# Pre-LN transformer layer on eight cores: per-tile tokens for the transposed activations, and the softmax scaling moved from VectorE to ScalarE

## The chip, the cores and the metric

The kernel runs as one program on all 8 cores of one Trainium2 chip (two dies, cores 0 to 3 and 4 to 7). The metric is the device time of the slowest core in microseconds (us). Each core has a matrix engine (TensorE, PE in the rows; PEld are its weight loads), VectorE (DVE), ScalarE (ACT), GpSimd (POOL), and SyncE (SP), which issues transfers.

## The reference

One layer with layer norm ahead of each half, cut to its core (4 sequences of 2048 tokens, width 2048, 16 heads of 128, 16 experts of width 1024, top 4, and a shared expert):

```python
x = x + attn(layernorm(x))        # scores = q k^T * 128**-0.5, causal, softmax, probs @ v, then @ Wo + bo
x = x + moe(layernorm(x))         # sigmoid router, top 4 renormalised, silu(x wg) * (x wu) @ wd, plus shared expert
```

The softmax is `exp(s) / sum(exp(s))` over the keys of a row. The division by the row sum is the scaling that this case moves.

## The kernel before

Two cores share one sequence. Each core takes 1024 query rows (every second row), and builds keys and values for all 2048 rows of its sequence. Weights are cast to bf16 on their way in. The program is four blocks of hand-ordered instructions. A small scheduler class (`Sched`) keeps one in-order list per engine and a table of tokens: an operation names the tokens it reads and writes, and gets a semaphore wait for the last writer of each token it reads (and for the readers of each token it writes). Nothing is reordered: what stands first in an engine's list runs first.

**Block 1, layer norm and transposes** (about 0 to 111 us). 16 tiles of 128 rows are loaded, normalised (`ln1_stats`, `ln1_norm`, L269 on ScalarE), transposed on TensorE into the four PSUM tiles `psLN` (`ln1_tp`, L280) and copied by VectorE into `ln1T` (`ln1_ev`, L288). All 32 copies write one token, `("lnT",)`.

**Block 2, attention** (about 112 to 1173 us). For each of 16 heads, `projall` (through `proj`, L347) makes q, k and v with 2 + 4 + 4 groups of 16 matmuls of 512 columns; ScalarE evicts each group (L351). `vtrans` transposes v (L459, L463). Then 8 query tiles k = 0 to 7 follow. Tile k has L = 256(k+1) keys, so L runs from 256 to 2048, in chunks of 512 or 256. For one tile:

- `s_front(k)`: per chunk a TensorE matmul into one of three banks of `psS` (L368), a VectorE minimum and mask in place (L376, L381, L386), and a ScalarE exp into `psb[k % 3]` (L391), whose row sum is read out by a second ScalarE instruction (ACTIVATION_READ_ACCUMULATOR, same line).
- `s_back(k)`: on VectorE the sum of the chunk sums (L404), the reciprocal (L407), and then the scaling of the whole row block `psb`, 128 x L, by the reciprocal, in place (L411).
- `pt_part(k)`: 2(k+1) TensorE transposes of `psb` into `psPT` (L424), evicted by ScalarE copies of up to 1024 columns into `ptb` (L429).
- `pv_part(k)`: 2(k+1) TensorE matmuls with v (L437); every fourth tile a ScalarE copy to `YT` (L444).

The tiles are software-pipelined by the order in which they are listed:

```python
for k in range(NST):
    s_front(k)
    if k >= 1: s_back(k - 1)
    if k >= 2: pt_part(k - 2)
    if k >= 3: pv_part(k - 3, h)
s_back(7)
if h + 1 < NH: projall(h + 1)      # and the prefetch of weights for head h + 2
pt_part(6); pv_part(5, h); pt_part(7); pv_part(6, h); pv_part(7, h)
```

**Blocks 3 and 4**: the output projection with `wo` (about 1173 to 1346 us; its weight loads wait for all that the engines did in attention), then the second layer norm with the router and the 17 expert passes (1458 us to the end) in one block. The change touches none of them.

Of the kernel before, what the change touches and what calls it, by code (L numbers as in the profile page):

```python
# [10 lines left out]
AF = mybir.ActivationFunctionType  # L11
ALU = mybir.AluOpType
# [139 lines left out]
def build_program():  # L152
# [22 lines left out]
    S = Sched()  # L175

    with ExitStack() as top:
# [5 lines left out]
        cst = E(nc.sbuf_tensor("cst", [128, 3], F32))  # L183
        onr = E(nc.sbuf_tensor("onr", [1, 128], BF16))
        st_ln = E(nc.sbuf_tensor("st_ln", [128, 16], F32))
        st_at = E(nc.sbuf_tensor("st_at", [128, 24], F32))
        bnr = E(nc.sbuf_tensor("bnr", [128, 48], F32))

        with ExitStack() as sAB:
# [3 lines left out]
            with ExitStack() as s1:  # L193
# [10 lines left out]
                with ExitStack() as p1:  # L204
# [5 lines left out]
                    psLN = [EP(nc.psum_tensor(f"psLN{j}", [128, 1024], BF16)) for j in range(4)]  # L210
# [8 lines left out]
                         writes=[("io32",)])  # L219
                    S.op("dve", lambda e, a=ident, b=io32: e.tensor_scalar(a[:], b[:], 0.0, None, ALU.is_equal),  # L220
                         reads=[("io32",)], writes=[("ident",)])
# [5 lines left out]
                         reads=[("bqtr",)], writes=[("bqts",)])  # L227

                    for nm, dst, src in (("wqb", wqb, d_wq), ("wkb", wkb, d_wk), ("wvb", wvb, d_wv)):
                        S.dma("pool", nm,  # L230
                              lambda e, o=dst, i=src: e.dma_start(out=o[:], in_=i[0], max_dma_last_dim=MDL),
                              writes=[(nm,)])
# [51 lines left out]
                    def ln1_ev(i):  # L284
                        for j in range(2):
                            bj = 2 * (i % 2) + j
                            S.op("dve", lambda e, p=psLN[bj], i=i, j=j:
                                 e.tensor_copy(ln1T[:, 8 * j:8 * (j + 1), i * 128:(i + 1) * 128],  # L288
                                               p[:].rearrange("p (a b) -> p a b", b=128)),
                                 reads=[("psLN", bj)], writes=[("lnT",)])  # L290

                    ln1_load(0)
                    ln1_load(1)
# [14 lines left out]
                    for k in range(NST):  # L308
# [3 lines left out]
                              writes=[("xr", k)])  # L312
# [6 lines left out]
                with ExitStack() as at:  # L319
# [5 lines left out]
                    psb = [EA(nc.sbuf_tensor(f"psb{s}", [128, 2048], BF16)) for s in range(3)]  # L325
# [9 lines left out]
                    def proj(h, wbuf, wtok, bias_ap, btok, scal, dst, dtok, nchunks, pp, stride2):  # L335
                        for ncx in range(nchunks):
                            p = psP[pp[0] % 2]
                            ptok = ("psP", pp[0] % 2)
                            pp[0] += 1
                            fns = []  # L340
                            for ct in range(NCT):
                                if stride2:
                                    rhs = lnr[:, ct, 4 * ncx:4 * ncx + 4, 0:256:2]
                                else:
                                    rhs = ln1T[:, ct, ncx * 512:(ncx + 1) * 512]
                                fns.append(lambda e, p=p, w=wbuf, ct=ct, rhs=rhs:
                                           e.matmul(p[:], w[:, ct, :], rhs,  # L347
                                                    start=(ct == 0), stop=(ct == NCT - 1)))
                            S.group("pe", fns, reads=[(wtok,), ("lnT",)], writes=[ptok])
                            S.op("act", lambda e, p=p, d=dst, ncx=ncx, b=bias_ap, sc=scal:  # L350
                                 e.activation(d[:, ncx * 512:(ncx + 1) * 512], p[:], AF.Identity,  # L351
                                              bias=b, scale=sc),
                                 reads=[ptok, btok], writes=[dtok + (ncx,)])
# [43 lines left out]
                    def s_back(k):  # L397
                        par = k % 2
                        pb = k % 3
                        base = 12 * par  # L400
                        L = 256 * (k + 1)
                        nchunks = len([512] * (L // 512) + ([256] if L % 512 else []))
                        S.op("dve", lambda e, base=base, nchunks=nchunks:
                             e.reduce_sum(st_at[:, base + 9:base + 10], st_at[:, base + 5:base + 5 + nchunks],  # L404
                                          axis=AX.X),
                             reads=[("sum", par, ci) for ci in range(nchunks)], writes=[("tsum", par)])
                        S.op("dve", lambda e, base=base: e.reciprocal(st_at[:, base + 10:base + 11],  # L407
                                                                     st_at[:, base + 9:base + 10]),
                             reads=[("tsum", par)], writes=[("at2", par)])
                        S.op("dve", lambda e, L=L, base=base, pb=pb:  # L410
                             e.tensor_scalar(psb[pb][:, 0:L], psb[pb][:, 0:L],  # L411
                                             st_at[:, base + 10:base + 11], None, ALU.mult),
                             reads=[("at2", par), ("psb", pb)], writes=[("psb", pb)])

                    def pt_part(k):
                        pb = k % 3
# [86 lines left out]
            with ExitStack() as wp:  # L503
# [7 lines left out]
                      writes=[("bo",)])  # L511
                for co in range(2):
# [3 lines left out]
                          writes=[("wob", co)])  # L516
                S.dma("pool", "wg", lambda e: e.dma_start(out=wg_b[:], in_=d_wgt[0], max_dma_last_dim=MDL),
                      writes=[("wg",)])
                S.dma("pool", "wu", lambda e: e.dma_start(out=wu_b[:], in_=d_wut[0], max_dma_last_dim=MDL),
                      writes=[("wu",)])  # L520
                for co in range(4):
                    sl = co % 2
                    if co >= 2:
# [3 lines left out]
                              writes=[("wob", sl)])  # L527
                    for m in range(NST):
                        fns = [lambda e, m=m, ct=ct, sl=sl: e.matmul(psW[m][:], YT[:, ct, m * 128:(m + 1) * 128],  # L529
                                                                     wo_b[sl][:, ct, :],  # L530
                                                                     start=(ct == 0), stop=False)
                               for ct in range(NCT)]
# [4 lines left out]
                                writes=[("psW", m)])  # L537
# [3 lines left out]
                             reads=[("psW", m), ("xr", m)], writes=[("xr", m)])  # L541
                S.flush(nc, semh)

        with ExitStack() as fp:
# [19 lines left out]
                  writes=[("gw",)])  # L564
            for hh in range(2):
# [4 lines left out]
                      writes=[("wd", hh)])  # L570
            S.dma("pool", "smp", lambda e: e.dma_start(out=ebr_sb[:], in_=d_ebr[:], max_dma_last_dim=MDL),
                  writes=[("ebr",)])
            S.level("smp", [("ebr",)])

            with ExitStack() as rp:
# [4 lines left out]
                     reads=[("onr",), ("ebr",)], writes=[("psR",)])  # L580
# [39 lines left out]
                for mt in range(NST):  # L620
# [6 lines left out]
                         reads=[("xr", mt)], writes=[("bnr2", sl, 0)])  # L627
                    S.op("dve", lambda e, x=xv, bb=bb: e.bn_stats(bnr[:, bb + 6:bb + 12], x[:, 512:1024]),  # L628
                         reads=[("xr", mt)], writes=[("bnr2", sl, 1)])
                    S.op("dve", lambda e, x=xv, bb=bb: e.bn_stats(bnr[:, bb + 12:bb + 18], x[:, 1024:1536]),  # L630
                         reads=[("xr", mt)], writes=[("bnr2", sl, 2)])
                    S.op("dve", lambda e, x=xv, bb=bb: e.bn_stats(bnr[:, bb + 18:bb + 24], x[:, 1536:2048]),  # L632
                         reads=[("xr", mt)], writes=[("bnr2", sl, 3)])
                    S.op("dve", lambda e, bb=bb, b=b: e.bn_aggr(st_ln[:, b:b + 2], bnr[:, bb:bb + 24]),
                         reads=[("bnr2", sl, 0), ("bnr2", sl, 1), ("bnr2", sl, 2), ("bnr2", sl, 3)],
                         writes=[c0])
                    S.op("act", lambda e, b=b: e.activation(st_ln[:, b + 2:b + 3], st_ln[:, b + 1:b + 2],  # L637
                                                            AF.Ln, bias=cst[:, 0:1], scale=1.0),
                         reads=[c0, ("cst",)], writes=[c1])
                    S.op("act", lambda e, b=b: e.activation(st_ln[:, b + 3:b + 4], st_ln[:, b + 2:b + 3],  # L640
                                                            AF.Exp, bias=cst[:, 1:2], scale=-0.5),
                         reads=[c1, ("cst",)], writes=[c1])
# [4 lines left out]
                         reads=[c0, c1], writes=[c2])  # L647
                    S.op("act", lambda e, x=xv, b=b:
                         e.activation(lnb2[:], x, AF.Identity, bias=st_ln[:, b + 4:b + 5],  # L649
                                      scale=st_ln[:, b + 3:b + 4]),  # L650
                         reads=[("xr", mt), c1, c2, ("lnb2",)], writes=[("lnb2",)])
                    for j in range(2):
                        fns = [lambda e, p=psL2[j], q=q, j=j:
                               e.transpose(p[:, q * 128:(q + 1) * 128],  # L654
                                           lnb2[:, (8 * j + q) * 128:(8 * j + q + 1) * 128], ident[:])
                               for q in range(8)]
# [4 lines left out]
                             reads=[("pl", j)], writes=[("x2t", mt, j)])  # L661
# [3 lines left out]
            with ExitStack() as xp:  # L665
# [5 lines left out]
                for e_i in range(NE + 1):  # L671
                    shared = (e_i == NE)
                    for th in range(2):
                        for which, wbuf, wtok, ps in (("g", wg_b, ("wg",), psG), ("u", wu_b, ("wu",), psU)):
                            for mi in range(8):
                                p = ps[mi % 2]
                                ptok = (f"ps{which}", mi % 2)
                                fns = [lambda e, p=p, w=wbuf, ct=ct, mi=mi, th=th:
                                       e.matmul(p[:], w[:, ct, mi * 128:(mi + 1) * 128],  # L679
                                                X2T[:, ct, th * 512:(th + 1) * 512],  # L680
                                                start=(ct == 0), stop=(ct == NCT - 1))
                                       for ct in range(NCT)]
# [6 lines left out]
                                if which == "g":  # L689
                                    S.op("act", lambda e, p=p, mi=mi: e.activation(g_sb[:, mi, :], p[:], AF.Silu,  # L690
                                                                                   bias=cst[:, 1:2], scale=1.0),
                                         reads=[ptok, ("cst",)], writes=[("gsb", mi)])
                                else:
                                    S.op("dve", lambda e, p=p, mi=mi: e.tensor_tensor(g_sb[:, mi, :], p[:],  # L694
                                                                                      g_sb[:, mi, :], ALU.mult),
                                         reads=[ptok, ("gsb", mi)], writes=[("gsb", mi)])
                        if th == 1 and e_i <= NE - 1:
                            nsrc_g = d_swgt if e_i == NE - 1 else d_wgt[e_i + 1]
                            S.dma("pool", "wg", lambda e, s=nsrc_g: e.dma_start(out=wg_b[:], in_=s, max_dma_last_dim=MDL),
                                  writes=[("wg",)])  # L700
                        for mtl in range(4):
                            mt = th * 4 + mtl
                            for co in range(4):
                                bnk = (mtl * 4 + co) % 4
                                p = psD[bnk]
                                fns = [lambda e, p=p, ic=ic, mtl=mtl, co=co:
                                       e.matmul(p[:], g_sb[:, ic, mtl * 128:(mtl + 1) * 128],  # L707
                                                wd_b[:, ic, co * 512:(co + 1) * 512],
                                                start=(ic == 0), stop=(ic == 7))
                                       for ic in range(8)]  # L710
                                S.group("pe", fns,
                                        reads=[("gsb", ic) for ic in range(8)] + [("wd", 0), ("wd", 1)],
                                        writes=[("psD", bnk)])
# [115 lines left out]
```

## Time and profile before

| | |
|---|---|
| times of the kernel before | 4324.37 and 4946.24 us; median 4635.31 us |
| the profiled execution, whole | 4326.25 us |
| its span on the slowest core (3) | 4324.6 us |
| TensorE busy | 3889.8 us, 90% of the span |
| VectorE busy | 1018.8 us, 24% |
| ScalarE busy | 802.6 us, 19% |
| GpSimd busy | 88.0 us, 2% |

The times are of one execution each. The profile is a separate execution, and all its rows are of core 3. Busy shares are means over stages that have different limits, so the rows below are of single stages. The other cores' spans are 4304.9 to 4321.6 us. The median stands between two executions that differ by 14%, and the profiled execution agrees with the lower of them.

### The profile page before, as it was taken

Reading aid. Unit: us, or ns where it says so; the run is one execution under the profiler, and the core shown is the slowest. Engines: PE = TensorE matmul, PEld = TensorE weight load, DVE = VectorE, ACT = ScalarE, POOL = GpSimd, SP = SyncE. Lnnn points to the kernel's source line nnn. Section 1 sums busy time; section 2 is a strip of 40 time slices with the busy share of each in tenths; the row PEclk is TensorE's granted clock in tenths of the full one; section 3 lists DMA queues with packets and bytes.
Section 4 is the critical chain, followed back from the end, with each engine's and each line's share of the span. In section 5 each row is a group of like instructions: output and inputs, shape, how many; then the busy total and the mean of one; then the engine's idle time right before and its main releaser. Section 6 shows DMA issues by size and latency. Waiting matters only on the chain.

```text
span 4324.6 us, 50288 instructions; the slowest of 8 cores (4304.9 to 4324.6 us)
## 1 busy us (share of the span) xinstructions
PE 3889.8 (90%) x19553; PEld 1832.6 (42%) x19553; DVE 1018.8 (24%) x1837; ACT 802.6 (19%) x1427; POOL 88.0 (2%) x129
## 2 busy tenths in 40 slices
PE   2888888878674699999999999999999999999999
PEld 2444444444332344444444444444444444444444
DVE  5132232232211221122122112212211221221122
ACT  3355454454401300000000000000000000000000
POOL 0000000000000000000000000000000000000000
PEclk9989889889887799999999999999999999999999
DMA  6311111111192043734725626527437347256261
GB/s 195 84 20 25 25 20 30 25 20 30 17 140 40 1 66 52 117 49 69 117 33 84 98 34 103 81 37 117 65 53 117 49 69 117 33 85 98 34 103 78
DMA packets 74100, 284.41 MB, mean 66 GB/s; under 512 B 2960, under 2 KB 11408, under 8 KB 69776
## 3 DMA queue, kind: packets, MB, share of 16 engines
q0 software_dynamic: 68832, 247.61, 35.6%
q1 hardware_dynamic: 5040, 33.58, 2.2%
q8 instruction: 165, 2.70, 0.2%
q14 instruction: 63, 0.52, 0.0%
HBM read 520.39 MB, written 8.39 MB: 122 GB/s over the span
## 4 chain that ended last, share of the span: by engine, by line
PE 66%; DVE 1%; ACT 1%; DMA 1%; issue 0%; POOL 0%; DVEq 0%; ACTq 0%; POOLq 0%
PE psD L707 22%; PE psG L679 22%; PE psU L679 22%; DMA ebr_sb<-ebr 1%; DVE g_sb L694 1%; ACT lnb L649 0%; PE psL L654 0%; ACT L637 0%; DVE X2T L659 0%; DVE bnr L626 0%; DVE bnr L632 0%; DVE bnr L630 0%; DVE bnr L628 0%; ACT st_ln L637 0%; ACT st_ln L640 0%
## 5 line engine op out<-in xcount | busy, mean ns | idle before, releaser
L707 PE MATMUL psD<-wd_b,g_sb 128*128 128x512 bf16 x4352 | 944.7, 379 | 35.8 <-DVE g_sb L694 35.8
L679 PE MATMUL psG<-X2T,wg_b 128*128 128x512 bf16 x4352 | 947.0, 380 | 0.0
L679 PE MATMUL psU<-X2T,wu_b 128*128 128x512 bf16 x4352 | 944.9, 379 | 0.0
L690 ACT ACTIVATE g_sb<-psG,cst 128x512 bf16<-128x512 f32 x272 | 186.9, 687 | 2611.9 <-PE psG L679 2611.9
L707 PEld LDWEIGHTS psD<-wd_b,g_sb 128*128 128x128 bf16 x4352 | 423.5, 98 | 557.1 <-issue 51.6
L679 PEld LDWEIGHTS psG<-X2T,wg_b 128*128 128x128 bf16 x4352 | 426.2, 98 | 514.9 <-issue 2.8
L679 PEld LDWEIGHTS psU<-X2T,wu_b 128*128 128x128 bf16 x4352 | 425.9, 98 | 513.4
L694 DVE TENSOR_TENSOR g_sb<-psU,g_sb 128x512 bf16<-128x512 f32 x272 | 188.1, 692 | 1682.5 <-PE psU L679 1682.5
L721 DVE SCALAR_TENSOR_TENSOR x_res<-psD,c_all,x_res 128x512 f32<-128x512 f32 x512 | 384.2, 750 | 540.6 <-PE psD L707 540.6
L368 PE MATMUL psS<-kt,qt 128*128 128x512 bf16 (+1 forms) x320 | 136.4, 468 | 116.6 <-ACT psb L391 53.3
L347 PE MATMUL psP<-ln1T,wvb 128*128 128x512 bf16 x1024 | 223.6, 379 | 0.0
L347 PE MATMUL psP<-ln1T,wkb 128*128 128x512 bf16 x1024 | 223.6, 379 | 0.0
L391 ACT ACTIVATE psb<-psS,cst 128x512 bf16<-128x512 f32 (+1 forms) x320 | 206.7, 647 | 49.2 <-DVE psS L386 18.8
L381 DVE SCALAR_TENSOR_TENSOR psS<-psS,mask_sb 128x256 f32<-128x256 f32 x128 | 55.0, 430 | 678.9 <-PE psS L368 670.9
L529 PE MATMUL psW<-wo_b,YT 128*128 128x512 bf16 x512 | 119.6, 388 | 41.8 <-DMA wo_b<-wo 41.8
L429 ACT COPY ptb<-psPT 128x1024 bf16<-128x1024 bf16 (+1 forms) x192 | 152.3, 794 | 12.1 <-PE psPT L424 1.0
L347 PEld LDWEIGHTS psP<-ln1T,wkb 128*128 128x128 bf16 x1024 | 100.1, 98 | 121.2
L347 PEld LDWEIGHTS psP<-ln1T,wvb 128*128 128x128 bf16 x1024 | 100.1, 98 | 120.9
L424 PE MATMUL psPT<-ident,psb 128*128 128x128 bf16 x1152 | 110.1, 251 | 40.8 <-ACT ptb L429 16.4
L347 PE MATMUL psP<-ln1T,wqb 128*128 128x512 bf16 x512 | 128.7, 411 | 1.4 <-PEq L124 1.4
L386 DVE TENSOR_SCALAR psS<-psS 128x512 f32<-128x512 f32 x192 | 127.1, 694 | 9.8 <-PE psS L368 8.0
L437 PE MATMUL psPV<-ptb,vsb 128*128 128x128 bf16 x1152 | 105.0, 246 | 14.8 <-ACT ptb L429 14.8
(95 smaller groups left out, 1137.2 us busy)
## 6 DMA issues: line engine op xcount, KB each, us to landing
wg_b<-wgt POOLq DMA_DIRECT2D x16, 4096.0 KB, 29.3
wu_b<-wut POOLq DMA_DIRECT2D x16, 4096.0 KB, 29.4
wd_b<-wdt POOLq DMA_DIRECT2D x32, 2048.0 KB, 22.9
xsl<-xkv SPq DMA_DIRECT2D x16, 1024.0 KB, 5.1
wqb<-wq POOLq DMA_DIRECT2D x16, 512.0 KB, 5.2
wkb<-wk POOLq DMA_DIRECT2D x16, 512.0 KB, 5.1
wvb<-wv POOLq DMA_DIRECT2D x16, 512.0 KB, 5.1
x_res<-xkv SPq DMA_DIRECT2D x8, 1024.0 KB, 18.9
```

The source lines that it names most:

```text
L347: e.matmul(p[:], w[:, ct, :], rhs, start=(ct == 0), stop=(ct == NCT - 1)))
L368: e.matmul(psS[:, bk * 512:bk * 512 + w], qt[:, k * 128:(k + 1) * 128], kt[:, off:off + w], start=True, stop=True)],
L386: e.tensor_scalar(psS[:, bk * 512:bk * 512 + w], psS[:, bk * 512:bk * 512 + w], 90.0, None, ALU.min),
L391: e.activation(psb[pb][:, off:off + w], psS[:, bk * 512:bk * 512 + w], AF.Exp, bias=cst[:, 2:3], scale=1.0, accum_out=st_at[:, base + 5 + ...
L424: e.transpose(pt[:, (j - r) * 128:(j - r + 1) * 128], psb[pb][:, j * 128:(j + 1) * 128], ident[:])
L429: e.copy(ptb[tb][:, r:r + n, :], pt[:, 0:n * 128].rearrange("p (a b) -> p a b", b=128)),
L529: fns = [lambda e, m=m, ct=ct, sl=sl: e.matmul(psW[m][:], YT[:, ct, m * 128:(m + 1) * 128], wo_b[sl][:, ct, :], start=(ct == 0), stop=Fals ...
L679: e.matmul(p[:], w[:, ct, mi * 128:(mi + 1) * 128], X2T[:, ct, th * 512:(th + 1) * 512], start=(ct == 0), stop=(ct == NCT - 1))
L690: S.op("act", lambda e, p=p, mi=mi: e.activation(g_sb[:, mi, :], p[:], AF.Silu, bias=cst[:, 1:2], scale=1.0), reads=[ptok, ("cst",)], writ ...
L694: S.op("dve", lambda e, p=p, mi=mi: e.tensor_tensor(g_sb[:, mi, :], p[:], g_sb[:, mi, :], ALU.mult), reads=[ptok, ("gsb", mi)], writes=[(" ...
L707: e.matmul(p[:], g_sb[:, ic, mtl * 128:(mtl + 1) * 128], wd_b[:, ic, co * 512:(co + 1) * 512], start=(ic == 0), stop=(ic == 7))
L721: e.scalar_tensor_tensor(x_res[:, mt, co * 512:(co + 1) * 512], p[:], c_all[:, mt, e_i:e_i + 1], x_res[:, mt, co * 512:(co + 1) * 512], AL ...
```

## The change

Two edits. In block 1 each of the 32 copies into `ln1T` now writes the token of its own row tile, and each projection group reads the tokens of the row tiles that its columns come from: tiles 0 to 7 or 8 to 15 for q, four tiles for each group of k and v. In `s_back` the scaling of `psb` by the reciprocal is issued on ScalarE as an Identity activation, with a zero bias from `cst[:, 1:2]` and the reciprocal as its scale, where it was a VectorE multiply.

```diff
@@ ln1_ev @@
-                                 reads=[("psLN", bj)], writes=[("lnT",)])
+                                 reads=[("psLN", bj)], writes=[("lnT", i)])
@@ proj @@
-                            S.group("pe", fns, reads=[(wtok,), ("lnT",)], writes=[ptok])
+                            if stride2:
+                                ln_toks = [("lnT", t2) for t2 in range(8 * ncx, 8 * ncx + 8)]
+                            else:
+                                ln_toks = [("lnT", t2) for t2 in range(4 * ncx, 4 * ncx + 4)]
+                            S.group("pe", fns, reads=[(wtok,)] + ln_toks, writes=[ptok])
@@ s_back @@
-                        S.op("dve", lambda e, L=L, base=base, pb=pb:
-                             e.tensor_scalar(psb[pb][:, 0:L], psb[pb][:, 0:L],
-                                             st_at[:, base + 10:base + 11], None, ALU.mult),
-                             reads=[("at2", par), ("psb", pb)], writes=[("psb", pb)])
+                        S.op("act", lambda e, L=L, base=base, pb=pb:
+                             e.activation(psb[pb][:, 0:L], psb[pb][:, 0:L], AF.Identity,
+                                          bias=cst[:, 1:2], scale=st_at[:, base + 10:base + 11]),
+                             reads=[("at2", par), ("psb", pb), ("cst",)], writes=[("psb", pb)])
```

## Rows read from the trace of the kernel before

**Rows 1.** Busy time by stretch, core 3: stretch, length, busy (count) per engine, granted clock.
```profile
core 3: us, PE busy (x) PEld busy (x) DVE busy (x) ACT busy (x) POOL busy (x), PEclk, DMA share, GB/s
615.40:639.20 23.80, 14.93 (x98) 8.55 (x95) 17.61 (x46) 20.45 (x51) 0.00 (x0) 0.73 0.00 1
639.20:678.90 39.70, 38.74 (x218) 18.79 (x215) 0.99 (x4) 11.34 (x16) 1.59 (x3) 0.99 0.22 39
1458.00:4324.60 2866.60, 2825.74 (x13065) 1275.66 (x13062) 600.23 (x838) 189.77 (x275) 52.04 (x64) 1.00 0.45 74
```
**Rows 2.** Waits of ScalarE, 113 to 1173 us: waiter, waited for, us in total, times, longest.
```profile
ACT psb L391 <- DVE psS L386: 18.8, 32, 0.9
ACT psb L391 <- DVE st_at L404: 5.7, 25, 0.3
```
**Rows 3.** ScalarE in time order within one head: start, duration, instruction, [idle before <-releaser].
```profile
618.40 0.21 ACT L391 ACTIVATION_READ_ACCUMULATOR psb<-psS,cst 128x1 f32 x1
619.56 0.69 ACT L391 ACTIVATE psb<-psS,cst 128x512 bf16<-128x512 f32 x1 [0.95 <-DVE psS L386]
...
622.34 0.69 ACT L391 ACTIVATE psb<-psS,cst 128x512 bf16<-128x512 f32 x1 [0.28 <-DVE st_at L404]
...
623.80 0.69 ACT L391 ACTIVATE psb<-psS,cst 128x512 bf16<-128x512 f32 x1 [0.20 <-DVE psS L386]
...
638.19 0.69 ACT L391 ACTIVATE psb<-psS,cst 128x512 bf16<-128x512 f32 x1 [0.15 <-DVE st_at L404]
```
**Rows 4.** VectorE in time order, same head, same columns.
```profile
618.30 0.16 DVE L407 RECIPROCAL st_at<-st_at 128x1 f32<-128x1 f32 x1
618.57 0.29 DVE L411 TENSOR_SCALAR psb<-psb,st_at 128x256 bf16<-128x256 bf16 x1
618.77 0.69 DVE L386 TENSOR_SCALAR psS<-psS 128x512 f32<-128x512 f32 x1
```
**Rows 5.** Instruction groups by shape: busy us, mean ns of one, idle before.
```profile
L411 DVE TENSOR_SCALAR psb<-psb,st_at 128x2048 bf16<-128x2048 bf16 x16 | 12.1, 753 | 1.7
L411 DVE TENSOR_SCALAR psb<-psb,st_at 128x256 bf16<-128x256 bf16 x16 | 4.6, 286 | 1.7
L269 ACT ACTIVATE lnb<-xsl,st_ln 128x2048 bf16<-128x2048 f32 x16 | 33.3, 2088 | 0.2 <-issue 0.2
L429 ACT COPY ptb<-psPT 128x1024 bf16<-128x1024 bf16 x96 | 96.6, 1006 | 5.0 <-PE psPT L424 1.0 <-ACT ptb L429 0.4
L429 ACT COPY ptb<-psPT 128x256 bf16<-128x256 bf16 x32 | 11.8, 368 | 2.3
```
**Rows 6.** ScalarE in time order, end of block 1: two normalisations back to back.
```profile
104.21 4.07 ACT L269 ACTIVATE lnb<-xsl,st_ln 128x2048 bf16<-128x2048 f32 x2
```
**Rows 7.** End of block 1: line L124 of TensorE's queue, then the timeline around it.
```profile
L124 PEldq EVENT_SEMAPHORE  x4: 51/51/51, 111.5 to 4324.6; - x4
...
110.62 0.69 DVE L288 COPY ln1T<-psLN 128x1024 bf16<-128x1024 bf16 x1 [0.17 <-PE psLN L280]
111.89 7.39 PE L347 MATMUL psP<-ln1T,wqb 128*128 128x512 bf16 x32 [1.39 <-PEq L124]
```
**Rows 8.** Last head, end of attention: ScalarE in time order.
```profile
1164.50 1.73 ACT L429 COPY ptb<-psPT 128x1024 bf16<-128x1024 bf16 x2
1166.56 4.24 ACT L429 COPY ptb<-psPT 128x1024 bf16<-128x1024 bf16 x4 [0.33 <-PE psPT L424]
```
**Rows 9.** q projection on TensorE: slowest and fastest of ten heads, then all (as rows 5).
```profile
172.38 8.92 PE L347 MATMUL psP<-ln1T,wqb 128*128 128x512 bf16 x32
...
837.39 7.39 PE L347 MATMUL psP<-ln1T,wqb 128*128 128x512 bf16 x32
...
L347 PE MATMUL psP<-ln1T,wqb 128*128 128x512 bf16 x512 | 128.7, 411 | 1.4 <-PEq L124 1.4
```
**Rows 10.** Granted clock in 3 us stretches of one head, columns as rows 1.
```profile
633.00:636.00 3.00, 0.75 (x2) 0.19 (x2) 2.04 (x4) 2.83 (x7) 0.00 (x0) 1.00 0.00 0
636.00:639.00 3.00, 2.57 (x22) 2.40 (x23) 1.56 (x5) 2.55 (x9) 0.00 (x0) 0.57 0.00 0
```

## Prediction before the run

> **What bounds the kernel now.** I read the busy time by stretch first, because the page's busy shares are means over stages with different limits. From 1458 us to the end TensorE is busy for 2825.74 of 2866.60 us [rows 1]. The change touches nothing there, so 2867 us of the time cannot move. Attention repeats one head of about 70.5 us, and a head has two halves. In the second, the projections (639.20 to 678.90 us), TensorE is busy for 38.74 of 39.70 us and VectorE for 0.99: this half is TensorE's. In the first, the eight query tiles (615.40 to 639.20 us), TensorE is busy for 14.93 of 23.80 us, VectorE for 17.61 and ScalarE for 20.45. So the engine that receives the moved work is the fullest in the only half in which that work is due.
>
> Busy shares don't prove that ScalarE sets the pace, so I read what it waits for. In the tiles part its two waits for VectorE come to 18.8 + 5.7 = 24.5 us over all of attention [rows 2], 1.5 us a head. In one head these are four gaps, 0.95 + 0.28 + 0.20 + 0.15 = 1.58 us [rows 3]; all else is back-to-back ScalarE work and its own short gaps. The reader is to see that what VectorE could give back by being relieved is at most 24.5 us in all, and that anything put on ScalarE beyond these gaps lengthens the head.
>
> **Edit 1, the tokens.** The first projection could start before the last `ln1T` copies only if nothing else held it. The row in front of it shows what does: it idles 1.39 us, released by TensorE's queue at L124, and not by VectorE; an event semaphore of that line stands at 111.5 us, behind the end of the last copy at 110.62 + 0.69 = 111.31 us [rows 7]. The engines meet at the end of each block (x4, one per block end), so at 111.5 us all 32 copies are done and every new wait is already met. Later heads read copies that are long past. Value 0. If the meeting were not binding, the gain would end at the 1.39 us, so the range is 0 to -1.4 us. No instruction or transfer is added.
>
> **Edit 2, removed from VectorE.** 128 multiplies, 8 a head, from 286 ns (L = 256) to 753 ns (L = 2048) [rows 5]. They are worth only the gaps above.
>
> **Edit 2, added to ScalarE.** 128 activations of 128 x L, bf16 to bf16 in SBUF, with a per-partition scale and bias. The trace has no such instruction on bf16 input. The nearest row is the normalisation L269, with the same function and operand kinds: 2088 ns for 2048 columns [rows 5]. The slope comes from the copies, (1006 - 368) / 768 = 0.831 ns a column [rows 5]. Two L269 in a row end 4.07 us after the first starts, so the second costs 4.07 - 2.09 = 1.98 us [rows 6], which is 1.70 + 0.28. A scaling inserted between other ScalarE work thus costs 0.28 + 0.000831 L us. The low bound takes the copy's fixed part: 0.368 - 0.213 = 0.155 us, less the same 0.1 us of overlap, 0.05 instead of 0.28. I take 0.28, since L269 carries the same operands and the copy carries none.
>
> The Trainium skill ("ScalarE: Activation LUTs", section "What ACT_TABLE_LOAD costs") gives 280 ns + 0.833 ns a column with a pointer bias, 93 ns more for a pointer scale, and an overlap of 93 ns between neighbours. L269 agrees: 2079 ns by that rule, 2088 measured. The same page's "Rules for kernel authors" would leave a multiply on VectorE, in bf16 up to about 3 times faster; the rows give 2088 against 753 ns at 2048 columns, 2.8 times.
>
> **Where the eight scalings of a head fall.** In ScalarE's list `s_back(k-1)` stands behind the exps of tile k, and ahead of the copies of `pt_part(k-2)` and the exps of tile k+1, which wait behind it.
> - k = 0 to 5 fall inside the tiles part. Their columns sum to 256(1+...+6) = 5376: 5376 x 0.831 ns = 4.47, and 6 x 0.28 = 1.68, together 6.15 us a head.
> - k = 6 and 7 (1.77 and 1.98 us) come after the last exp. What follows on TensorE is the projection of the next head, which needs ScalarE first for an eviction some 4 us in, and the projections leave ScalarE 39.70 - 11.34 = 28 us free [rows 1]. Hidden, cost 0, in 15 heads. In the last head no projection covers them: the two copies at 1164.50 wait for the first, the four copies at 1166.56 for both [rows 8], and the barrier and weight loads of `wo` follow. Gross 1.77 + 1.98 = 3.75; 0.33 us of that is idle already, so +3.4 us, once.
>
> **What the gaps give back, a head.** The 0.95 us gap stands where tile 2's first exp waits for VectorE's minimum. The reciprocal ends at 618.30 + 0.16 = 618.46; then VectorE does the multiply, 0.29 us, and only then the minimum from 618.77 to 619.46 [rows 4]. With the multiply gone the minimum starts about 0.28 us earlier, and the k = 0 scaling (0.49 us) runs on ScalarE in the gap that is left (0.95 - 0.28 = 0.67): 0.28 + 0.49 = 0.77 us back. The three small gaps (0.63 us) close, as ScalarE reaches those exps later than before and VectorE sooner. Sum 1.40 us a head; low bound 0.77.
>
> TensorE loses nothing: its transposes of tile k-1 come an iteration later, when the scaling is long done, and its waits in this part are already for ScalarE. The reciprocal is no new wait either: it is ready 0.4 us after the last mask, within the last exp.
>
> **Sum.** 16 x (6.15 - 1.40) = 76.0; plus 3.4 for the last head; plus 0 for edit 1: +79.4 us. On the profiled execution, 4326.25 + 79.4 = 4405.7 us, 1.8% more. The median before, 4635.31 us, is half way to an execution of 4946.24 us, and I predict the undisturbed level of the profiled execution and of the 4324.37 us.
>
> **The clock.** The granted clock is 1.00 at 633 us, where TensorE hardly works, and 0.57 at 636 to 639 us, after that pause [rows 10]; between the levels 1.2 and 2.4 GHz. The q projection starts on it: 7.39 us in the fastest head and 8.92 in the slowest, 128.7 / 16 = 8.04 on average [rows 9]. The pauses of TensorE ahead of the last tile's matmuls grow by the scaling inserted there, so the low clock can be met in more heads. Bounds: all heads as the slowest, 15 x 0.88 = +13 us; all as the fastest, 15 x -0.65 = -10 us. I take 0, as the mean of 8.04 already lies between the two and nothing here says which way the meeting of pause and projection will drift.
>
> **The rivals.**
> - *Dearer.* The same mechanism, but the three small gaps stay (16 x 0.63 = +10) and the projections all start as the slowest (+13): 4405.7 + 23 = 4429 us. For it: TensorE's pauses grow. Against it: VectorE has slack by then. With only 7.1 us more than my sum it passes 2% (4412.8 us).
> - *Cheaper scaling.* The fixed part is the copy's: 16 x 6 x 0.23 = -22, 4384 us. For it: bf16 input from SBUF is not in the rows. Against: the operands are those of L269.
> - *Not slower.* VectorE's queue, not ScalarE, paces the tiles (minimum, mask, sum, reciprocal and multiply lie in one line), and the scalings disappear in ScalarE's slack. It would return the whole 24.5 us: 4326.25 - 24.5 + 3.4 = 4305 us. It needs 6.15 us of slack on ScalarE in each tiles part; it has 23.80 - 20.45 = 3.35, of which 1.58 in waits on VectorE. It decides only where ScalarE has more idle time than the scaling costs.
> - *No effect.* Scalings and gains cancel, 4326 us; this needs the same slack.
>
> **How the numbers follow.** Chances: my sum 0.53; dearer 0.32; cheaper 0.09; not slower or no effect 0.04; anything else 0.02. About 2% is what a measurement of this kernel can tell from no change. My sum, cheaper, and the two rivals without loss lie within it: 0.66, less 0.01 for a gain larger than any mechanism I find. The dearer rival lies beyond it, with half of the unnamed: 0.33. Faster gets 0.02, since even a perfect relief of VectorE is 0.6%. The range is from the cheaper rival less 8 us of clock, 4376, to the dearer plus 9 us for what I mis-sized, 4438. It leaves out the cases without loss.
>
> **What the profile after would show.** VectorE has no L411 and is 66 us less busy (128 at the middle of 286 and 753 ns). ScalarE has 128 Identity activations on `psb`, about 0.60 us at L = 256 and 2.09 at 2048, on average 1.34, some 172 us in all. A tiles part lasts 28.5 us instead of 23.8, a projections part 39.7 as before, a head about 75.3. ScalarE's waits for VectorE nearly vanish, and TensorE's waits for `psb` grow. The first projection still starts behind L124. The stretch of the experts stays 2867 us. I am wrong if the activations come out much under 0.5 us at L = 256, if the tiles part grows by less than the scalings inside it minus 1.6 us, or if the projections part changes length.

## The result

| | before | changed |
|---|---|---|
| median of all runs | 4324.86 us (10 runs) | 4502.98 us (11 runs) |
| lowest run | 4323.95 us | 4416.67 us |
| ratio, changed to before | | 1.0216, 95% interval 1.0202 to 1.0231 |
| profiled execution, span of the slowest core | 4324.6 us | 4416.1 us |
| ScalarE busy | 802.6 us | 958.0 us |
| VectorE busy | 1018.8 us | 953.9 us |

The change makes the kernel 2.2% slower, about 93 us on 4325. Seven of the eleven executions of the changed kernel had one die or both at a lower mean granted clock; the ratio leaves them out, and the median of 4502.98 us, which lies outside the forecast range of 4376 to 4438 us, does not.

The first view is the busy time by stretch of the changed kernel, core 2: one tiles part, and the experts. The columns are those of [rows 1].

```profile
core 2: us, PE busy (x) PEld busy (x) DVE busy (x) ACT busy (x) POOL busy (x), PEclk, DMA share, GB/s
720.80:749.20 28.40, 16.16 (x93) 9.41 (x92) 14.12 (x38) 25.95 (x55) 0.00 (x0) 0.57 0.00 1
1548.80:4416.10 2867.30, 2812.02 (x12794) 1275.48 (x13054) 600.28 (x838) 189.69 (x275) 52.05 (x64) 1.00 0.40 74
```

The experts take 2867 us, as in [rows 1]. The tiles part has grown from 23.8 to 28.4 us, ScalarE in it from 20.45 to 25.95 us busy, and VectorE has fallen from 17.61 to 14.12. TensorE's mean granted clock there was 0.73 and is 0.57.

The groups by shape show the moved instructions, which stand at line L415 now, and the nearest row of before, L269.

```profile
L415 ACT ACTIVATE psb<-psb,cst,st_at 128x2048 bf16<-128x2048 bf16 x16 | 33.5, 2095 | 0.0
L269 ACT ACTIVATE lnb<-xsl,st_ln 128x2048 bf16<-128x2048 f32 x16 | 33.3, 2087 | 0.2 <-issue 0.2
...
L415 ACT ACTIVATE psb<-psb,cst,st_at 128x256 bf16<-128x256 bf16 x16 | 9.6, 600 | 0.6 <-DVE st_at L411 0.6
```

They cost 2095 and 600 ns against 2.09 and 0.60 us forecast, and bf16 input makes no difference to the f32 of L269. None waits for anything except the smallest, 0.6 us in all.

Who waits for whom, 113 to 1250 us of the changed kernel (waiter, waited for, us in total, times, longest):

```profile
ACT psb L395 <- DVE st_at L408: 3.1, 15, 0.5
...
PE psS L372 <- ACT psb L395: 99.6, 50, 3.8
PE psPT L428 <- ACT ptb L433: 66.1, 78, 1.4
```

The same row of the kernel before, 113 to 1173 us:

```profile
PE psS L368 <- ACT psb L391: 53.3, 45, 2.2
```

ScalarE's waits for VectorE, 24.5 us in [rows 2], are down to 3.1 + 0.6 (the smallest scaling's). TensorE waits for exps 99.6 us instead of 53.3, and its longest pause has grown from 2.2 to 3.8 us.

ScalarE in time order, from the last exp of tile 1 to the first of tile 2, and later from the last row sum of tile 6 on (start, duration):

```profile
723.70 0.21 ACT L395 ACTIVATION_READ_ACCUMULATOR psb<-psS,cst 128x1 f32 x1
723.85 0.60 ACT L415 ACTIVATE psb<-psb,cst,st_at 128x256 bf16<-128x256 bf16 x1
724.49 0.69 ACT L395 ACTIVATE psb<-psS,cst 128x512 bf16<-128x512 f32 x1
...
741.91 0.19 ACT L395 ACTIVATION_READ_ACCUMULATOR psb<-psS,cst 128x1 f32 x1
742.00 1.66 ACT L415 ACTIVATE psb<-psb,cst,st_at 128x1536 bf16<-128x1536 bf16 x1
743.56 1.51 ACT L433 COPY ptb<-psPT 128x1024 bf16<-128x1024 bf16 x2
...
748.60 0.69 ACT L395 ACTIVATE psb<-psS,cst 128x512 bf16<-128x512 f32 x1 [0.51 <-DVE st_at L408]
```

The k = 0 scaling sits in the old gap: from row sum to exp it was 1.16 us in [rows 3] and is 0.79 with the scaling inside. The k = 5 scaling delays the copies behind it by 743.56 - 742.00 = 1.56 us, which is 0.28 + 0.000831 x 1536 to the hundredth.

The part that the sum did not hold is the clock of TensorE. Granted clock (the figure ahead of the last two) in 3 us stretches of one head of the changed kernel, to be read beside [rows 10]:

```profile
725.00:728.00 3.00, 1.89 (x10) 0.88 (x9) 1.75 (x6) 2.71 (x9) 0.00 (x0) 0.50 0.00 0
...
743.00:746.00 3.00, 0.35 (x1) 0.00 (x0) 1.50 (x3) 2.86 (x5) 0.00 (x0) 0.50 0.00 0
746.00:749.00 3.00, 2.51 (x21) 2.34 (x22) 1.09 (x4) 2.20 (x7) 0.00 (x0) 0.50 0.01 3
749.00:752.00 3.00, 3.00 (x11) 1.23 (x10) 0.32 (x2) 3.00 (x4) 0.00 (x0) 0.50 0.00 0
752.00:755.00 3.00, 3.00 (x14) 1.24 (x13) 0.00 (x0) 2.86 (x4) 0.00 (x0) 1.00 0.00 0
```

From 725 to 752 us the clock stays at its lower level, 1.2 GHz. In the head of the kernel before in [rows 10] it had come back to 1.00 in the middle of the tiles, at 633 us. The first 3 us of the q projection (from 749.2) run at half speed in this head.

### The profile page after: what moved, and what is told of

Read it like the earlier page. It is cut to its first block, busy times and chain, and to the rows that moved or that the text cites. A ratio compares the mean times of both kernels' runs of the same rounds, so it can differ in the third digit from the quotient of the medians.

```text
span 4416.1 us, 49913 instructions; the slowest of 8 cores (4399.3 to 4416.1 us)
## 1 busy us (share of the span) xinstructions
PE 3902.7 (88%) x19199; PEld 1851.5 (42%) x19553; DVE 953.9 (22%) x1709; ACT 958.0 (22%) x1555; POOL 88.0 (2%) x129
## 3 DMA queue, kind: packets, MB, share of 16 engines
HBM read 520.39 MB, written 8.39 MB: 120 GB/s over the span
## 4 chain that ended last, share of the span: by engine, by line
PE 64%; DVE 1%; issue 1%; ACT 1%; DMA 1%; POOL 0%; DVEq 0%; ACTq 0%; POOLq 0%
PE psD L711 21%; PE psG L683 21%; PE psU L683 21%; DVE g_sb L698 1%; DMA ebr_sb<-ebr 1%; ACT lnb L653 0%; PE psL L658 0%; ACT L641 0%; DVE X2T L663 0%; DVE bnr L630 0%; DVE bnr L636 0%; DVE bnr L634 0%; DVE bnr L632 0%; ACT st_ln L641 0%; ACT st_ln L644 0%
## 5 line engine op out<-in xcount | busy, mean ns | idle before, releaser
L372 PE MATMUL psS<-kt,qt 128*128 128x512 bf16 (+1 forms) x289 | 142.2, 529 | 132.7 <-ACT psb L395 99.6
L347 PE MATMUL psP<-ln1T,wvb 128*128 128x512 bf16 x1006 | 222.7, 379 | 0.9
L347 PE MATMUL psP<-ln1T,wkb 128*128 128x512 bf16 x1008 | 222.7, 379 | 0.8
L428 PE MATMUL psPT<-ident,psb 128*128 128x128 bf16 x1152 | 120.8, 267 | 85.4 <-ACT ptb L433 69.6
L415 ACT ACTIVATE psb<-psb,cst,st_at 128x256 bf16<-128x256 bf16 (+7 forms) x128 | 171.3, 1338 | 0.6 <-DVE st_at L411 0.6
L347 PEld LDWEIGHTS psP<-ln1T,wkb 128*128 128x128 bf16 x1024 | 100.2, 98 | 121.1
L347 PEld LDWEIGHTS psP<-ln1T,wvb 128*128 128x128 bf16 x1024 | 100.3, 98 | 120.7
L428 PEld LDWEIGHTS psPT<-ident,psb 128*128 128x128 bf16 x1152 | 94.1, 119 | 120.0 <-issue 115.8
```

What stands on the lines that cost most here:

```text
L347: e.matmul(p[:], w[:, ct, :], rhs, start=(ct == 0), stop=(ct == NCT - 1)))
L372: e.matmul(psS[:, bk * 512:bk * 512 + w], qt[:, k * 128:(k + 1) * 128], kt[:, off:off + w], start=True, stop=True)],
L415: e.activation(psb[pb][:, 0:L], psb[pb][:, 0:L], AF.Identity, bias=cst[:, 1:2], scale=st_at[:, base + 10:base + 11]),
L428: e.transpose(pt[:, (j - r) * 128:(j - r + 1) * 128], psb[pb][:, j * 128:(j + 1) * 128], ident[:])
```

## The experiments

**Theory A.** ScalarE's queue sets the pace of the tiles part; the loss is the scalings that fall into it, less the gaps, and the token edit is dead. From the unread matmuls on it has a clock part, taken from the changed kernel's trace: TensorE's low granted clock lengthens what stands at the end of the tiles and the q projection. **Rivals.** B: the tokens carry part of the loss. C: every activation costs its own time wherever it stands. D: VectorE's queue paces the tiles. E: the clock doesn't matter. F: the part behind the projections is TensorE's, not ScalarE's.

### The first edit alone

```diff
 # changed kernel, with the scaling back on VectorE; tokens ("lnT", i) kept
-                        S.op("act", ... e.activation(psb[pb][:, 0:L], ..., scale=st_at[:, base + 10:base + 11]) ...)
+                        S.op("dve", ... e.tensor_scalar(psb[pb][:, 0:L], ..., None, ALU.mult) ...)
```

> Only the first edit: one token per row tile of ln1T; the scaling stays on VectorE. Theory A (ScalarE's queue takes all of the loss, the tokens are dead because the engines meet at the end of block 1): 4325 us, ratio 0.999 to 1.001, first projection still released by TensorE's queue at L124. Rival B (the tokens add or save waits that matter): it would have to carry part of the +92 us, so above 1.005, or gain the 1.4 us idle time at the block's end in every run.

Ratio 0.9999 (0.9986 to 1.0012), as theory A expects and below B's 1.005. The end of block 1 in its trace, line L124 of TensorE's queue and the first projection:

```profile
L124 PEldq EVENT_SEMAPHORE  x4: 51/51/51, 110.2 to 4322.4; - x4
...
110.83 2.76 PE L347 MATMUL psP<-ln1T,wqb 128*128 128x512 bf16 x6 [1.66 <-PEq L124]
```

The first projection is still released by the meeting of the engines and not by a copy, as in [rows 7]. A gain as small as 1.4 us could not be told by the ratio; that there is none is read from this row.

### The second edit alone

```diff
 # kernel before, with the scaling on ScalarE; one token ("lnT",) kept
-                        S.op("dve", ... e.tensor_scalar(psb[pb][:, 0:L], ..., None, ALU.mult) ...)
+                        S.op("act", ... e.activation(psb[pb][:, 0:L], ..., scale=st_at[:, base + 10:base + 11]) ...)
```

> Only the second edit: the scaling on ScalarE for all k, tokens as before. Theory A: the whole loss, ratio 1.020 to 1.023, about 4417 us. Rival B: clearly less than the whole change's 1.0216.

Ratio 1.0217 (1.0188 to 1.0247), against the whole change's 1.0216. B falls.

### Only the scalings behind the last exp

```diff
+                        if k >= 6:
+                            S.op("act", ... AF.Identity ...)      # as in the change
+                        else:
+                            S.op("dve", ... ALU.mult ...)         # as before
```

> The scaling on ScalarE only for k = 6 and 7, the two that stand behind the last exp of a head; k = 0 to 5 stay on VectorE. Theory A (place decides: these two are covered by the next head's projections except in the last head): +3.4 us, ratio 1.000 to 1.002, 4328 us. Rival C (each activation costs its own time wherever it stands): 16 x (1.77 + 1.98) = +60 us, ratio 1.014.

Ratio 1.0008 (0.9992 to 1.0024). The interval excludes the 1.014 of C: 16 x (1.87 + 2.10) = 63 us of activation time cost at most about 10, and the head keeps its length (next section). The last head, where no projection covers them, ScalarE on core 3:

```profile
1169.60 0.19 ACT L391 ACTIVATION_READ_ACCUMULATOR psb<-psS,cst 128x1 f32 x1
1169.69 1.87 ACT L412 ACTIVATE psb<-psb,cst,st_at 128x1792 bf16<-128x1792 bf16 x1
1171.46 1.73 ACT L435 COPY ptb<-psPT 128x1024 bf16<-128x1024 bf16 x2
1173.09 2.10 ACT L412 ACTIVATE psb<-psb,cst,st_at 128x2048 bf16<-128x2048 bf16 x1
1175.08 1.94 ACT L435 COPY ptb<-psPT 128x1024 bf16<-128x1024 bf16 x2
```

From the first instruction behind the last row sum to the copies of tile 6 it is 1175.08 - 1169.69 = 5.39 us; in [rows 8] it is 1166.56 - 1164.50 = 2.06. Up to that point the tail is 3.3 us longer, against the 3.4 forecast. Followed to the last copy into `YT` it is less on most cores: from the last exp to that copy, two cores of the kernel before take 8.37 us (core 3 is one) and six take 9.48, and all cores of the changed kernel 11.59, so 3.2 us more on two cores and 2.1 on six.

### No scaling at all

The softmax stays unnormalised here: the 128 multiplies are gone, while the sum and the reciprocal stay.

```diff
-                        S.op("dve", ... e.tensor_scalar(psb[pb][:, 0:L], ..., None, ALU.mult) ...)
```

> The scaling is left out altogether (sum and reciprocal stay), so the softmax is not normalised. Theory A (ScalarE paces the tiles): only the gaps in which ScalarE waits for VectorE can close, 16 x 0.28 = 5 us to 24.5 us less, 4301 to 4320 us, ratio 0.994 to 0.999. Rival D (VectorE's queue paces the tiles): the six multiplies of k = 0 to 5, 16 x 2.7 = 43 us less, 4281 us, ratio 0.990.

Ratio 0.9984 (0.9972 to 0.9996), 7 us less. Freeing VectorE of all 128 multiplies (66 us) returns 7, and ScalarE's two waits for VectorE, 24.5 us in [rows 2], still come to 10.4 + 6.7 us. The interval excludes D's 0.990.

### Unread matmuls in TensorE's pauses

```diff
+                            nfill = {6: 5, 7: 7}.get(k, 0) if ci == nchunks - 1 else 0   # changed kernel
+                            # in the kernel before: {6: 2, 7: 5}
+                            if nfill:
+                                S.group("pe", [lambda e, k=k: e.matmul(psP[0][:], qt[:, k * 128:(k + 1) * 128],
+                                               kt[:, 0:512], start=True, stop=True) for _ in range(nfill)],
+                                        reads=[("qt", k // 4), ("kt", 0)], writes=[("psP", 0)])
```

> The changed kernel, plus matmuls whose result nobody reads, in TensorE's pauses: 5 of 128x512 ahead of the last chunk of tile 6 and 7 ahead of that of tile 7, into a psP bank that is free there; 12 x 16 matmuls more. Theory A with a clock part (the low granted clock of 0.50 lasts from tile 2 into the q projection, and costs 1.3 us at the end of the tiles and 1.2 us in the q projection of each head): the clock is back at 1.00 before the q projection, q projection 7.2 to 7.5 us where it was 8.4, tiles part 25.3 to 26.6; 4380 to 4400 us, ratio 1.013 to 1.018. Rival E (the clock does not matter, the excess over the forecast is ScalarE's own): 4417 us or more, ratio 1.0216 or above, q projection as before.

> The kernel before, with the same kind of matmuls: 2 ahead of the last chunk of tile 6 and 5 ahead of that of tile 7. Theory A with a clock part: every head gets the full clock at the end of its tiles, which now only some have: tiles part 21.5 to 20.5 us, q projection 7.9 to 7.3: 16 x 1.6 = 26 us less, 4299 us, ratio 0.993 to 0.996. Rival E: no gain, ratio 1.000 or above.

On the changed kernel the ratio to the kernel before is 1.0166 (1.0144 to 1.0188), where it was 1.0216. On the kernel before it is 0.9947 (0.9929 to 0.9965). Both add work to TensorE, and each is faster than the same kernel without it; E falls. One expectation was missed: the q projection of the changed kernel was to fall to 7.2 to 7.5 us and is 7.87 on average (table below), since it starts at the full clock in some heads only. TensorE at the end of the tiles, first in the changed kernel (core 2), then in the changed kernel with the unread matmuls (L374; core 5):

```profile
746.49 0.58 PE L372 MATMUL psS<-kt,qt 128*128 128x512 bf16 x1 [3.13 <-ACT psb L395]
746.87 1.48 PE L428 MATMUL psPT<-ident,psb 128*128 128x128 bf16 x12
748.15 1.27 PE L441 MATMUL psPV<-ptb,vsb 128*128 128x128 bf16 x10
749.22 8.71 PE L347 MATMUL psP<-ln1T,wqb 128*128 128x512 bf16 x31
```

```profile
732.07 1.67 PE L374 MATMUL psP<-kt,qt 128*128 128x512 bf16 x7
735.99 0.38 PE L380 MATMUL psS<-kt,qt 128*128 128x512 bf16 x1 [2.25 <-ACT psb L403]
736.21 0.83 PE L436 MATMUL psPT<-ident,psb 128*128 128x128 bf16 x12
736.87 0.72 PE L449 MATMUL psPV<-ptb,vsb 128*128 128x128 bf16 x10
737.43 4.91 PE L347 MATMUL psP<-ln1T,wqb 128*128 128x512 bf16 x21
```

The granted clock is 0.50 in the first view and 1.00 in the second. The same 12 transposes take 1.48 us at the lower level and 0.83 at the full one, the 10 matmuls with v 1.27 and 0.72. From the last score matmul to the q projection it is 749.22 - 746.49 = 2.73 us against 737.43 - 735.99 = 1.44. That is 1.3 us, all of it in front of the projection and none of it covered. In the kernel before with the unread matmuls the longest q matmul takes 388 ns, where it took 634. Line L347 on the slowest core of that kernel, q (duration min/median/max in ns, first and last start), then the same of the kernel before and of the changed one:

```profile
L347 PE MATMUL psP<-ln1T,wqb x512: 386/387/388, 110.7 to 1079.5; 128*128 128x512 bf16 x171
```

```profile
L347 PE MATMUL psP<-ln1T,wqb x512: 386/387/634, 111.9 to 1106.1; 128*128 128x512 bf16 x171
```

```profile
L347 PE MATMUL psP<-ln1T,wqb x496: 386/387/634, 111.9 to 1187.8; 128*128 128x512 bf16 x166
```

### Work moved the other way

The second copy of each pair of transposes goes from ScalarE to VectorE: in the first kernel for tiles 6 and 7 and for v, all behind the projections; in the second for tiles 4 and 5 too.

```diff
+                            if ri == 1 and k >= 6:                # second kernel: if ri == 1
+                                S.op("dve", ... e.tensor_copy(ptb[tb][:, r:r + n, :], ...), writes=[("ptb", tb, ri)])
+                            else:
                                 S.op("act", ... e.copy(ptb[tb][:, r:r + n, :], ...), writes=[("ptb", tb, ri)])
```

> The kernel before, with work moved the other way, from ScalarE to VectorE: the second copy of the transposes of tiles 6 and 7 and of v, behind the projections, where VectorE is idle. Theory A (ScalarE's queue sets the time outside the projections): the copies of a pair run side by side, 2 to 3 us less a head, 4277 to 4293 us, ratio 0.989 to 0.993. Rival F (this part is TensorE's, its waits for copies are 29 us in all): no more than 0.5 us a head, ratio 0.998 or above.

> As the one before, and also the second copies of tiles 4 and 5, within the tiles part. Theory A: ScalarE loses another 0.7 us a head in the part where it is full, 11 us less than the kernel with the tail alone, 4266 to 4285 us. Rival D (VectorE is close to full there): no gain over the tail alone, or a loss.

Ratio 0.9929 (0.9912 to 0.9947) for the tail alone, at the edge of what A expected. The second kernel has too few times for a ratio. Its two lowest are 4285.28 and 4285.40 us, against a lowest of 4290.69 for the first, and its trace shows a head 0.44 us shorter, of which 0.24 in the tiles part (the table below), where 0.7 were expected. F, 0.998 or above, falls.

> The kernel before with both gains: the second copies of each pair on VectorE in all tiles and for v, and the unread matmuls ahead of the last chunks of tiles 6 and 7. Theory A with a clock part: the two act on different time, so they add: about -38 us for the copies and -23 us for the clock, 4262 us, ratio 0.985 to 0.988. If both buy the same pauses of TensorE: not under 0.990.

> As the one before, and the only copy of tile 3 (1024 columns) on VectorE too. Theory A: ScalarE loses 0.9 us a head in the tiles part, VectorE gets 0.6: up to 14 us less than without it. Rival D (VectorE has no room left there): no gain or a loss.

The split copies of the second kernel with the unread matmuls {6: 2, 7: 5}: 0.9871 (0.9855 to 0.9886), lowest run 4267.71 us, median 4270.85. Most of the two gains adds: a head is 3.65 us shorter, where 2.60 for the copies and 1.67 for the clock would make 4.27. With tile 3's only copy on VectorE as well (`if ri == 1 or k == 3`) it is 0.9877 (0.9856 to 0.9898) and the lowest run 4272.06 us, no gain. Waits of ScalarE for VectorE's minimum in this one:

```profile
ACT psb L399 <- DVE psS L394: 28.3, 46, 1.4
```

Without tile 3's copy the same row reads 12.9 us. Here D begins to hold: ScalarE is spared 16 x 0.9 = 14 us of copies and waits 15 us more for minimums that VectorE does later.

### One scaling into the gap

```diff
+                        if k == 0:
+                            S.op("act", ... AF.Identity ...)      # as in the change
+                        else:
+                            S.op("dve", ... ALU.mult ...)         # as before
```

> The kernel before with only the scaling of k = 0 on ScalarE. Theory A (that one falls into the gap in which ScalarE waits for VectorE's minimum, and shortens it): 0.3 to 0.4 us less a head, -5 us, ratio 0.998 to 1.000. Rival C (each activation costs its own 0.5 us): +8 us, ratio 1.002.

Ratio 0.9992 (0.9977 to 1.0007). C's 1.002 is excluded, but the expected gain of 5 us is not told apart from none. The trace shows the gap closing: the two waits of [rows 2], 24.5 us in all, are 5.2 + 2.2 us here.

## Where the head's time went

To put numbers on the parts of a head, I took from the timelines of all eight cores the first start of the q projection, of the k projection and of the first exp in each head, and averaged over heads and cores. Each row is one execution. Three stretches: tiles (first exp to q projection), q projection, and the rest (k and v projections, last tiles of the head before, v transposes).

```text
kernel                              tiles   q proj   rest    head (us)
before                              21.49    7.91    36.72   66.12
changed                             26.63    8.39    36.57   71.59
first edit alone (tokens)           21.33    7.70    36.72   65.74
second edit alone (scaling)         26.58    8.47    36.57   71.61
k = 6, 7 on ScalarE only            21.45    7.91    36.57   65.93
no scaling                          21.10    7.75    36.62   65.47
k = 0 on ScalarE only               21.23    7.80    36.88   65.91
changed + unread matmuls            25.70    7.87    36.57   70.14
before + unread matmuls             20.50    7.23    36.72   64.45
before, tail copies split           20.93    7.90    35.13   63.96
before, all second copies split     20.69    7.69    35.14   63.52
the same + unread matmuls           20.11    7.23    35.13   62.47
that + tile 3's copy on VectorE     20.29    7.22    35.16   62.67
```

The changed head is 5.47 us longer. The rows of line L347 above give the same: (1187.8 - 1106.1) / 15 = 5.45 us a head. With 16 tiles parts and the longer last tail that is 5.14 x 16 + 0.48 x 15 - 0.15 x 15 + 3.3 = 90.5 us, or 89 with the tail of most cores; the spans of the two profiles differ by 91.5.

The first edit alone shows how far two executions of the same work differ. Its engines run what they ran before, yet its head is 0.38 us shorter, all of it in the tiles and the q projection, the two stretches that hang on the clock. Differences of that size in the table's first two columns, such as those of k = 0 and of k = 6, 7, are therefore not told apart from none. The third column does not scatter like this: it is 36.72 in both. (The 36.88 of k = 0 comes from two cores alone.)

## Why the prediction came out as it did

**What held.** The forecast was 4405.7 us, 79.4 us more. It was made for the level of the profiled execution, and there the ratio puts the changed kernel at 1.0216 x 4325 = 4418 us. The direction and the mechanism on ScalarE are right, and that time lies within the range of 4376 to 4438 us; the increase was 93 us, 14 more than forecast.
- Edit 1 at zero, because the engines meet at L124: shown by the first edit alone (0.9999) and by its row.
- The price of one scaling, 0.28 + 0.000831 L us: 600 and 2095 ns, and 1.56 us of delay at L = 1536.
- Place decides: shown by k = 6 and 7 alone (1.0008), with 2.1 to 3.3 us in the last head, where 3.4 were forecast.
- VectorE's relief is nearly worthless: shown by the run without scaling (-7 us).
- The rival in which VectorE paces the tiles is excluded for this kernel. It starts to hold only once ScalarE has been relieved (tile 3's copy).

**What failed.** The step "The clock. I take 0" was mis-sized: between the two profiled executions the clock is worth about +12 us. It has two parts.
- The q projection, the only part that the step had in its bounds, went from 7.91 to 8.39 us: 15 x 0.48 = 7 us, about half of the +13 at the upper bound. Not all heads came out as the slowest.
- The last transposes and v matmuls in front of the q projection were not in the sum at all. They are on the path too, and take 1.3 us more at the lower clock. In the kernel before, two kinds of tiles parts stand side by side: 27 of 120 (15 heads on eight cores) near 20.5 us, with the full clock at their end, and 93 near 21.8. In the changed kernel 89 of 120 are near 26.55 us, 26 longer (26.8 to 27.2), and only 5 shorter. The lost full-clock heads are 21.79 - 21.49 = 0.30 us a head, 5 us.

That the two parts together come near the upper bound of the one is chance. The rest of the tiles part is as forecast: 26.55 - 21.79 = 4.76 us a head, where the sum had 6.15 - 1.40 = 4.75. The longer ones among the changed kernel's tiles parts add 26.63 - 26.55 = 0.08 us a head, 1 us, and the "rest" stretch gives 0.15 us a head back, 2 us. So 79 + 7 + 5 + 1 - 2 = 90 us, against the 91.5 between the two spans. The unread matmuls show the clock as the cause: they take 1.45 us a head out of the changed kernel without touching ScalarE's list. Its size is less sure. Set against the execution of the first edit alone, whose q projections (7.70 us) and tiles parts (21.33) met the full clock more often, the same two parts would be 15 x 0.69 + 16 x 0.46 = 18 us.

The reason given for taking 0 was that nothing says which way the low clock will drift. The prediction's own sentence pointed one way: TensorE's pauses grow. Ahead of the last chunk they went from 1.4 to 2.2 us before to 3.1 to 3.8 us in every head, and its busy share of the tiles part fell from 63% to 57%. Over the last 3 us before the q projection the mean granted clock is above 0.95 in 23 of 120 heads before and in none of the changed kernel. A term above 0 was the better choice; that it would come to about 12 us could not be had from the rows.

**The rivals.** None came out as written. Of the dearer one (4429 us), the three small gaps mostly closed (3.1 us in all are left of its 10), and 7 of its 13 us of clock came. The cheaper fixed part is excluded by the 1.56 us of delay, which holds the full 0.28.

**Two smaller slips.** The four gaps: the first gave back more than written (1.16 to 0.79 us with the scaling inside, so 0.37 instead of 0.28), while the last did not always close. It is 0.2 us on average over the 15 waits in the trace and 0.51 in the head shown, where the last score matmul (0.58 us at the lower clock) and its minimum come late. And a head is 66.1 us, not "about 70.5": no row gives that figure, and the two stretches of [rows 1] add up to 63.5 us because they leave out the end of the head. The forecast of a difference did not hang on it, but the "75.3 us head" did, and it was 71.6. The ends of those stretches are rough too: the second one holds, besides the projections (to about 674 us), 4 us of the last tiles.

What stays open: the 0.15 us a head in the rest, and what lies behind the last head. The 0.15 us goes with the scalings of k = 6 and 7, since it is there with these two alone (36.57), and 0.13 of it lies between the first of the four copies behind the projections (L429) and the copy into `YT`, 5.68 us before and 5.55 in the two kernels that have these scalings on ScalarE; why is not shown. Behind attention the same stretch varies by 15 us over the cores of the kernel before (3137 to 3152 us), so the 1 or 2 us missing from the sum can't be placed.

## What to carry to other kernels

- Before moving work between engines, take the fuller engine of the stretch where it will run, not of the whole program: ScalarE was at 19% of the kernel and at 86% of the stretch that mattered. The same instruction cost 0 behind the projections and its full issue interval in the tiles.
- A wait that grows on TensorE is not free because TensorE wasn't the bound: look whether its next dense stretch starts at the lower granted clock, and price the instructions just ahead of that stretch as well (here 1.3 us a head).
- In this kernel it pays to move work from ScalarE to VectorE, up to the point where VectorE's minimums come late: splitting pairs of evictions gave 0.7%, and seven unread matmuls a head 0.5%, together 1.3% below the kernel before.

## What the runs showed of the hardware

An Identity activation with pointer scale and bias costs the same on bf16 from SBUF as on f32 (2095 and 2087 ns for 2048 columns). The Trainium skill ("ScalarE: Activation LUTs", section "What ACT_TABLE_LOAD costs") has one rate for both types, and the trace agrees.

I had not expected that adding 112 matmuls of 128x512 to the kernel makes it 0.5% faster. With them the granted clock is 1.00 at the start of the q projection in all 15 heads on all cores (386 to 388 ns for the 512 q matmuls of the slowest core, where the longest took 634), and the tiles parts fall to one length, 20.5 us, where the kernel before mixes 20.5 and 21.8.
